# Scatter of three bfloat16 parts in one product, left terms from blocks that DMA brings into fixed slots

## What is computed

```python
idx = concatenate([edge_index, edge_index[:, ::-1]])      # 400,000 x 2
src, dst = idx[:, 0], idx[:, 1]
gl = (h @ Wl.T).reshape(N, 4, 16)[src]                    # "left" term
gr = (h @ Wr.T).reshape(N, 4, 16)[dst]                    # "right" term, gathered
score = (att * leaky_relu(gl + gr, 0.2)).sum(-1)          # 4 heads an edge
m = segment_max(score, src)
ex = exp(score - m[src])
denom = segment_sum(ex, src)
out = segment_sum(gr * (ex / denom[src]), src)            # N x 64
x = x + mlp(concatenate([out, h]))
# then: x = x + batchnorm(mlp(segment_sum(h2[src] + edge_attr, dst)))
```

## Time and profile before

| | |
|---|---|
| median of 3 runs | 9489.05 us (9473.34 to 9510.54) |
| the profiled execution's own time | 9484.91 us |
| its span | 9483.1 us |
| POOL busy | 5015.6 us (53%) |
| DVE busy | 4090.3 us (43%) |
| PE busy, PEld busy | 3658.2 us (39%), 3222.2 us (34%) |
| ACT busy | 260.2 us (3%) |
| TensorE clock granted in attention | 0.50 in every window shown below |

### The profile page before, as it was taken

How to read it: one execution, slowest core, us unless ns; L and a number is a source line. 1 busy time by engine, 2 the same in 40 slices (tenths; PEclk the granted TensorE clock), 3 DMA queues, 4 the chain that set the end, 5 groups by cost and what they waited for, 6 DMA issues and landing times. The chain is left out here.

```text
span 9483.1 us, 86794 instructions
## 1 busy us (share of the span) xinstructions
PE 3658.2 (39%) x21987; PEld 3222.2 (34%) x21988; DVE 4090.3 (43%) x6783; ACT 260.2 (3%) x352; POOL 5015.6 (53%) x4913
## 2 busy tenths in 40 slices
PE   1011112344444444444444434445463333334445
PEld 1011112343343334343333334334363333333344
DVE  8999823343444343434444344435441122222222
ACT  3011000000000000000000000000010000000000
POOL 0000065656565656556565656565417777676664
PEclk9975555555555555555555555555565555555555
DMA  2000022323232322223232223233711121111111
GB/s 21 0 0 0 26 59 68 80 78 81 69 84 74 79 76 80 72 72 83 67 88 76 77 69 83 75 77 84 66 55 46 43 45 45 44 44 44 43 44 34
DMA packets 442077, 557.62 MB, mean 59 GB/s; under 512 B 172858, under 2 KB 176058, under 8 KB 441698
## 3 DMA queue, kind: packets, MB, share of 16 engines
q1 hardware_dynamic: 281298, 391.72, 13.7%
q0 software_dynamic: 156672, 160.75, 10.8%
q10 hardware_dynamic: 3984, 3.89, 0.2%
HBM read 439.99 MB, written 115.95 MB: 59 GB/s over the span
## 5 line engine op out<-in xcount | busy, mean ns | idle before, releaser
L821 POOL DMA_INDIRECT rows<-gr_table,stage x3328 | 3385.3, 1017 | 3225.4 <-DVE stage L986 2227.2
L1303 POOL DMA_INDIRECT message<-h_table,edge_stage x1568 | 1614.7, 1030 | 783.9 <-issue 466.8
L883 PE MATMUL bank<-terms,hot_sum 128*128 128x68 f32 x6656 | 1610.3, 412 | 777.8 <-issue 753.4
L871 PE MATMUL bank<-gl_parts,hot_t 128*128 x10080 | 953.9, 236 | 2286.5 <-issue 2175.9
L883 PEld LDWEIGHTS bank<-terms,hot_sum 128*128 128x128 f32 x6656 | 1517.7, 326 | 828.8 <-issue 818.2
L871 PEld LDWEIGHTS bank<-gl_parts,hot_t 128*128 128x128 bf16 x10080 | 706.8, 127 | 2549.6 <-issue 2542.5
L1007 DVE TENSOR_TENSOR z<-bank,rows 128x512 f32<-128x512 f32 x416 | 286.6, 689 | 2761.4 <-remote 2618.6
L1330 PE MATMUL bank<-message,edge_hot 128*128 128x64 f32 x3136 | 720.4, 424 | 1463.1 <-DVE message L1375 1368.6
L1330 PEld LDWEIGHTS bank<-message,edge_hot 128*128 128x128 f32 x3136 | 683.5, 330 | 1499.9 <-DVE message L1375 1403.3
L1359 DVE TENSOR_TENSOR agg<-agg,bank 128x64 f32 x196 | 43.4, 221 | 1231.7 <-remote 737.1
L1015 DVE TENSOR_TENSOR hot_sum<-iota_row,place 128x1024 f32<-128x1024 f32 x416 | 506.8, 1218 | 25.7 <-PE bank L883 25.5
(11 more groups left out here) (254 smaller groups left out, 2320.5 us busy)
## 6 DMA issues: line engine op xcount, KB each, us to landing
place_b<-place_rows SPq DMA_DIRECT2D x422, 256.0 KB
gr_rows<-rows SPq DMA_DIRECT2D x416, 256.0 KB
rows_again<-gr_rows SPq DMA_DIRECT2D x416, 256.0 KB
rows<-gr_table,stage POOLq DMA_INDIRECT x3328
edge<-in_edge_attr SPq DMA_DIRECT2D x195, 256.0 KB
message<-h_table,edge_stage POOLq DMA_INDIRECT x1568
pen_s<-pen_rows ACTq DMA_DIRECT2D x56, 64.0 KB
gr_table<-gr SPq DMA_DIRECT2D x1, 1536.0 KB
```

The lines of the kernel that those rows point to most:

```text
L821: pool.indirect_dma_start(rows[k][:, g, :], None, m.gr_table[:, :], bass.IndirectOffsetOnAxis(stage[k][:, g:g + 1], 0)).then_inc(s_gath[k] ...
L871: last = pe.matmul(bank[slot][:, g * D:(g + 1) * D], hot_t[slot][:, g * P:(g + 1) * P], m.gl_parts[:, bass.ds(blks[g // GROUP_TILES], 1), ...
L883: last = pe.matmul(sums_of(slot, i), hot2[slot][:, g, :], terms[slot][:, g * HEADS:(g + 1) * HEADS, :].rearrange("p h w -> p (h w)"), star ...
L1303: pool.indirect_dma_start(rows[k][:, e, :], None, m.h2_table[:, :], bass.IndirectOffsetOnAxis(stage[k][:, e:e + 1], 0)).then_inc(s_gath[k] ...
```

## The change

Four edits that belong together.

1. `gl_parts` isn't kept on chip. Prepare writes it to a new HBM table `gl_table` [block, partition, 3 x 64], with three DMAs behind the store of `gr_table`. In attention SP reads two block numbers a step and loads the two blocks into one of 8 fixed slots `gl_step` (384 bytes a partition and block), six steps ahead. PE's left products read these slots at fixed addresses, and PE reads no block numbers.
2. The scatter's `terms` are split in three bfloat16 parts: ACT copies the high part, DVE subtracts it (`rest`), ACT copies the middle part, DVE subtracts it into the low part. `hot_sum` becomes bfloat16. A product of a tile then has 3 x 68 = 204 bfloat16 columns, 8 products a step, and `acc` has three sums for each block, added together once at the start of the node layer.
3. PE waits once a step (`s_parts`, or `s_hot` in the first chunk) in place of its waits on hot_t, z, terms and acc.
4. DVE's order within a step is new: z, terms and its weight column, first accumulate, hot_t, leaky, second accumulate, rest, hot_sum, weighed, stage, the low part, reduce. Several tiles share memory (`z` and `leaky` with `fore`, `weighed` and a piece of `rest` with `top`).

```diff
+        m.gl_table = nc.dram_tensor("gl_table", (BLOCKS, P, 3 * D), BF16).ap()
-        m.acc = sb("acc", [P, BLOCKS, HEADS * ACCW], F32)
+        m.acc = sb("acc", [P, BLOCKS, 3, HEADS * ACCW], F32)
-        m.gl_parts = sb("gl_parts", [P, BLOCKS, 3 * D], BF16, layer0)
...
@@ prepare, sync
-            sp.wait_ge(s_grt, 32)
+            sp.wait_ge(s_gl_parts, 1)
+            for part, piece in enumerate(gl_parts):
+                sp.dma_start(m.gl_table[:, :, part * D:(part + 1) * D].rearrange("b p f -> p b f"), piece).then_inc(s_grt, 16)
+            sp.wait_ge(s_grt, 80)
...
@@ attention
+    gl_s = [sb(f"gl_step{k}", [P, STEP_GROUPS, 3 * D], BF16, ctx) for k in range(U)]
-    hot2 = [sb(f"hot_sum{k}", [P, STEP_TILES, P], F32, ctx) for k in range(LAG)]
+    hot2 = [sb(f"hot_sum{k}", [P, STEP_TILES, P], BF16, ctx) for k in range(LAG)]
+    parts = [sb(f"parts{k}", [P, STEP_TILES, 3, HEADS * ACCW], BF16, ctx) for k in range(LAG)]
...
@@ sync
+            def load_left(q, slot):
+                for i in range(STEP_GROUPS):
+                    blk = sp.value_load(m.blk_i[0:1, bass.ds(q * STEP_GROUPS + i, 1)], min_val=0, max_val=BLOCKS - 1)
+                    sp.dma_start(gl_s[slot][:, i, :], m.gl_table[bass.ds(blk, 1), :, :].rearrange("b p f -> p (b f)")
+                                 ).then_inc(s_gl[slot], 16)
                     if part.score:
                         load_place(q + LAG + 2, (k + LAG + 2) % V)
+                        load_left(q + LAG + 2, (k + LAG + 2) % U)
...
@@ tensor
-                blks = [pe.value_load(m.blk_i[0:1, bass.ds(q * STEP_GROUPS + i, 1)], min_val=0, max_val=BLOCKS - 1)
-                        for i in range(STEP_GROUPS)]
-                pe.wait_ge(s_hot, q + 1)
-                at_least(pe, s_z, q - LAG + 1)
+                pe.wait_ge(s_gl[slot], loads * 16 * STEP_GROUPS)
                 for g in range(STEP_TILES):
                     for part in range(3):
-                        last = pe.matmul(bank[slot][:, g * D:(g + 1) * D], hot_t[slot][:, g * P:(g + 1) * P],
-                                         m.gl_parts[:, bass.ds(blks[g // GROUP_TILES], 1), part * D:(part + 1) * D
-                                                    ].rearrange("p b f -> p (b f)"),
+                        last = pe.matmul(bank[slot % LAG][:, g * D:(g + 1) * D], hot_t[slot % LAG][:, g * P:(g + 1) * P],
+                                         gl_s[slot][:, g // GROUP_TILES, part * D:(part + 1) * D],
                                          start=part == 0, stop=part == 2)
...
-            def scatter(r, slot):
-                pe.wait_ge(s_terms, r + 1)
-                at_least(pe, s_acc, STEP_GROUPS * (r - LAG + 1))
-                for i in range(STEP_GROUPS):
-                    for g in range(i * GROUP_TILES, (i + 1) * GROUP_TILES):
-                        last = pe.matmul(sums_of(slot, i), hot2[slot][:, g, :],
-                                         terms[slot][:, g * HEADS:(g + 1) * HEADS, :].rearrange("p h w -> p (h w)"),
+            def scatter(slot):
+                for g in range(STEP_TILES):
+                    last = pe.matmul(sums_of(slot, g // GROUP_TILES), hot2[slot][:, g, :],
+                                     parts[slot][:, g, :, :].rearrange("p w f -> p (w f)"),
...
+                    if part.sum:
+                        pe.wait_ge(s_parts, q - CHUNK_STEPS + 1)
+                    else:
+                        pe.wait_ge(s_hot, q + LAG + 1)
...
@@ scalar
+                    act.wait_ge(s_terms, r + 1)
+                    nc.scalar.copy(parts[k % LAG][:, :, 0, :], terms_by_tile).then_inc(s_hi, 1)
+                    act.wait_ge(s_rest, r + 1)
+                    nc.scalar.copy(parts[k % LAG][:, :, 1, :], rest[:, :, :]).then_inc(s_mid, 1)
...
@@ vector
+                        dve.wait_ge(s_hi, r + 1)
+                        dve.tensor_tensor(rest[:, :, :], terms_by_tile, parts[k % LAG][:, :, 0, :], ALU.subtract
+                                          ).then_inc(s_rest, 1)
                         dve.tensor_tensor(hot2[k % LAG][:, :, :], places, at, ALU.is_equal)
...
+                        dve.wait_ge(s_mid, r + 1)
+                        dve.tensor_tensor(parts[k % LAG][:, :, 2, :], rest[:, :, :], parts[k % LAG][:, :, 1, :], ALU.subtract
+                                          ).then_inc(s_parts, 1)
...
@@ attention_nodes
+            for w in (2, 1):
+                chain.link(dve.tensor_tensor(m.acc[:, :, w - 1, :], m.acc[:, :, w - 1, :], m.acc[:, :, w, :], ALU.add))
```

More of the change, by code:

```diff
@@ L431, in _ @@
             for part in range(3):
-                piece = m.gl_parts[:, :, part * D:(part + 1) * D]
+                piece = gl_parts[part]
                 c.link(dve.tensor_copy(piece, gl[:, :, :]))
@@ L721, in attention @@
     hot_t = [sb(f"hot_t{k}", [P, STEP], BF16, ctx) for k in range(LAG)]
-    hot2 = [sb(f"hot_sum{k}", [P, STEP_TILES, P], F32, ctx) for k in range(LAG)]
[L723 to L726, removed]
+    gl_s = [sb(f"gl_step{k}", [P, STEP_GROUPS, 3 * D], BF16, ctx) for k in range(U)]
+    hot2 = [sb(f"hot_sum{k}", [P, STEP_TILES, P], BF16, ctx) for k in range(LAG)]
+    fore = sb("fore", [P, SCAN], F32, ctx)
+    z, leaky = (fore[:, i * SW:(i + 1) * SW].rearrange("p (g f) -> p g f", f=D) for i in range(2))
+    wide = sb("wide", [P, SW + STEP_TILES * HEADS * ACCW], F32, ctx)
+    top = wide[:, 0:SCAN]
+    weighed = wide[:, 0:SW].rearrange("p (g f) -> p g f", f=D)
+    rest = wide[:, SW:].rearrange("p (g w) -> p g w", g=STEP_TILES)
+    terms = sb("terms", [P, PAIRS, ACCW], F32, ctx)
+    parts = [sb(f"parts{k}", [P, STEP_TILES, 3, HEADS * ACCW], BF16, ctx) for k in range(LAG)]
     scores = sb("scores", [P, CHUNK_TILES, HEADS], F32, ctx)
@@ L755, in attention @@
     s_place = [sem(f"s_place{k}") for k in range(V)]
+    s_gl = [sem(f"s_gl{k}") for k in range(U)]
     s_hot = sem("s_hot")
+    s_hi, s_rest, s_mid, s_parts = sem("s_hi"), sem("s_rest"), sem("s_mid"), sem("s_parts")
     s_step = sem("s_step")
@@ L849, in _ @@
                 load_place(q, q % V)
+                load_left(q, q)
             def turn(part):
@@ L926, in _ @@
             for q in range(LAG):
-                left(q, q).then_inc(s_step, 1)
+                pe.wait_ge(s_hot, q + 1)
+                left(q, 1).then_inc(s_step, 1)
             def turn(part):
@@ L948, in _, with body @@
             load_pens(0)
+            def body(part, j, first):
+                if not part.sum:
+                    return
+                for k in range(U):
+                    r = U * j + k - CHUNK_STEPS
+                    act.wait_ge(s_terms, r + 1)
+                    nc.scalar.copy(parts[k % LAG][:, :, 0, :], terms_by_tile).then_inc(s_hi, 1)
+                    act.wait_ge(s_rest, r + 1)
+                    nc.scalar.copy(parts[k % LAG][:, :, 1, :], rest[:, :, :]).then_inc(s_mid, 1)
             def turn(part):
                 c = part.c
+                if part.sum:
+                    loop(act, part, body)
                 if not part.score:
@@ L1008, in body @@
                                           rows[k][:, :, :], ALU.add).then_inc(s_z, 1)
+                    if part.sum:
+                        weight = weights[:, bass.ds(tile, STEP_TILES), :].rearrange("p g h -> p (g h)")
+                        dve.wait_ge(s_load[k % V], place_loads(j - outer, k))
+                        dve.tensor_tensor(terms[:, :, 0:DH],
+                                          rows2[k % V][:, :, :].rearrange("p g (h f) -> p (g h) f", f=DH),
+                                          weight.unsqueeze(2).to_broadcast([P, PAIRS, DH]), ALU.mult)
+                        dve.tensor_copy(terms[:, :, DH:ACCW], weight.unsqueeze(2)).then_inc(s_terms, 1)
+                    if add:
+                        accumulate(r - LAG, k % LAG, 0)
+                    if part.score:
                         hot_of(q + LAG, k % LAG, (k + LAG) % V, place_loads(j, k + LAG))
```

55 lines of the change are left out of this document (27 added, 28 removed).

## The result

The changed kernel takes 9341.44 us (median of 4 runs, 9317.39 to 9365.21) where the kernel before takes 9484.07 (4 runs beside them): a ratio of 0.9845, 95% interval 0.9805 to 0.9886. Forecast were 9325. The profiled execution took 9319.15 us, span 9317.3. So 166 us went between the two profiled executions, 143 between the medians, where 162 were forecast. But the parts of that sum came out quite different, so that the agreement is luck, and the last experiments make it likely that the sign itself hangs on a condition that lies outside the kernel.

A forecast was written before the change was run, and what follows sets the result against it. POOL was taken to wait for DVE and DVE for PE, slow at starting instructions. 9484.9 - 109 (short waits) - 240 (chunk ends) + 104 (gathers) + 83 (fixed costs) = 9323, rounded 9325 us; range 8550 to 9810.

The forecast's parts named there:

- What bounds the kernel: Attention: POOL waits for DVE, DVE for PE, which lacks its rate of starting instructions; 1,263 us of waits.
- I take a quick stretch to end after so many PE records, not after a time: Attention: a quick stretch holds 240 PE records, so 3.75 steps at 64 records, and a cycle grows from four steps to 5.7.
- the rival's fixed time: Attention: PE is quick for 16 us in all, to about 8 us after POOL's restart, whatever it has to start; chance 0.30.
- my -109: POOL's short waits for stage inside chunks: 74 become 52 at 10.6 us each, 551 us for 660.
- Chunk ends: POOL's waits at the 12 chunk ends: 20 us less each, -240 us in all, 0 to -500 possible.
- Gathers: POOL's gathers stretched by the two subtracts: +0.25 us a step, +104 us over 416 steps.
- Fixed costs: Prepare +15, memset and sum additions +12, last chunk +20, wider accumulations and longer last step at chunk ends +36: +83 us.
- Hidden work: ACT's copies (0.56 us each, up to 0.7) and SP's gl loads: nothing added to the time.
- The crawl is gone: Rival, chance 0.24: without the register-addressed operand PE no longer crawls in attention and POOL bounds all, 8579 us.
- POOL held up by DVE: Rival, chance 0.10: the two subtracts delay gathers by their whole length, 570 us for 104, total 9789 us.
- the likeliest: Main case, chance 0.36: fewer crawls, cycles of 5.7 steps, 9323 us, own range 9050 to 9480.
- Slower: Rival, chance 0.30: quick stretches are bounded by time, DVE fits 2.3 steps in place of 3, 9839 us.

The follow-up runs named there:

- e3: The changed kernel with 8 more bfloat16 products a step whose sums nobody reads, 80 records instead of 64: 9429.84 us, ratio 0.9807 to the kernel before.
- e6: The changed kernel's order, single wait and left slots, but float32 scatter products, no parts, copies or subtracts: 9605.59 us, ratio 0.9984 to the kernel before.
- e8: The changed kernel with VectorE's two subtracts cut to 8 columns each: 9446.95 us, ratio 0.9782 to the kernel before.
- e11: The kernel before, with POOL clearing 320 columns of an unused tile after every second gather: 8835.05 us, ratio 1.0758 to the kernel before (8213.67 us there).
- e1: The kernel before with only the left part changed (gl blocks by DMA into fixed slots): 9613.63 us, ratio 1.0007 to the kernel before.
- e2: The changed kernel with TensorE's left operand again addressed by registers, read from memory twice a step: 9437.84 us, ratio 0.9814 to the kernel before.
- e12: The changed kernel with subtracts cut to 8 columns each and two 512-column reduces of a constant in their places: 8425.48 us, ratio 1.0243 to the kernel before.
- e5: The kernel before with hot_sum and terms as bfloat16 tiles, leaving out the terms' middle and low part: 9328.58 us, ratio 0.9674 to the kernel before.
- e9: The kernel before, with POOL clearing a few bytes of an unused tile after every second gather: 9564.82 us, ratio 0.9955 to the kernel before.

## Why the forecast held, and where it did not

The time was right (9325 for 9341) and the sign was right. That the time is so near is luck: four terms were off by 285, 153, 182 and 53 us, some one way and some the other. The mechanism was half right. Point by point:

- *What bounds the kernel.* Right: the wait that ended last was POOL for VectorE for PE, and PE lacked a rate of starting instructions, not work time. What I did not see is that SyncE, and VectorE when it has work, share the beat. I had named the mark by which I would be wrong in the main: PE's issue waits not following its records. They did not (2176 and 2164 us; 2101 in e3).
- *The step that failed* is "I take a quick stretch to end after so many PE records, not after a time". In the changed kernel neither it nor the rival's fixed time is so: 16 more records change nothing (e3), and quick stretches went from 16 us to about 90. There a crawl begins when VectorE has caught up with POOL: behind the first chunk POOL is about one step ahead or less at its start. That is no rule for the kernel before, whose crawls begin with POOL nearly five steps ahead and 14 us after its restart; there the forecast's count of records and the rival's fixed time both still stand. So the forecast took the changed kernel to keep the old kind of quick stretch, and it went over to another. What brings that about is shown only in part: it took both the bfloat16 products (e6 without them keeps the short cycle, but has 80 records and no subtracts too) and the two subtracts at full length (e8). Why, stays open. Hence -394 us for my -109.
- *Chunk ends.* -87 us for -240. A crawl almost always falls on the chunk's last steps, so VectorE comes into the scan nearly as late as before (waits of up to 49 us, where the kernel before had up to 54).
- *Gathers.* The kind was right, the size was not: +286 us for +104. The next fence shows why: VectorE's two-operand work of a step stands nearly in a row, and this gather, started beside it, ends only when the row does.

```profile
3793.12 0.99 POOL L836 DMA_INDIRECT rows<-gr_table,stage  x1 [0.30 <-issue]
...
3794.13 1.21 DVE L1064 TENSOR_TENSOR hot_sum<-iota_row,place 128x1024 bf16<-128x1024 f32 x1
...
3794.41 2.36 POOL L836 DMA_INDIRECT rows<-gr_table,stage  x1 [0.30 <-issue]
3795.27 0.68 DVE L1067 TENSOR_TENSOR wide<-fore,att_sb 128x512 f32<-128x512 f32 x1
3795.87 0.16 DVE L1020 TENSOR_SCALAR stage<-row_of 128x8 int32 x1
3795.94 0.71 DVE L1073 TENSOR_TENSOR parts<-wide,parts 128x544 bf16<-128x544 f32 x1
3796.58 0.67 DVE L136 TENSOR_REDUCE scores<-wide 128x512 f32 x1
```

  The gather of 3794.41 ends at 3796.77, just past the end of the low part's subtract (3796.65) and inside the reduce that follows, which reads one operand. It is no single case: of the 378 gathers over 1.3 us, 281 end 0.1 us behind the low part's subtract. Beside no VectorE work a gather takes 0.94 us in both kernels (mean of 1606 after, of 1998 before); beside some, 1.25 us in the changed one, 1.13 before. My 0.58 us from 3.3 us of such work is 0.18 us a us; the same ratio is 0.27 here, 1.28 us from 4.7. The Trainium skill (SBUF — State Buffer, "SBUF: two separate sides") says that such an operation and a GpSimd one lock each other out wholly; this fence agrees with it better than the 0.94 to 1.43 on which I doubted it.
- *Fixed costs.* +30 us for +83. Prepare: nothing, not +15; the casts to bfloat16, whose output is no longer strided, took 1.79 us each and not 3.42, and the stores were through by 184, ahead of POOL's next work at 189.83. Last turn: 3.91 us a step for my 4.0 (3.41 before).
- *Hidden work.* Right: ScalarE's copies (0.645 us) made VectorE wait 2.8 us in all, the gl loads made PE wait in three places, 48 us. VectorE's quick step is 6.5 us where I had 7.0 (two starts of z, written to `fore`):

```profile
3790.65 0.67 DVE L1041 TENSOR_TENSOR fore<-bank,rows 128x512 f32<-128x512 f32 x1
...
3797.18 0.67 DVE L1041 TENSOR_TENSOR fore<-bank,rows 128x512 f32<-128x512 f32 x1
```

- *The rivals.* "The crawl is gone" gave 8579 us. The change did not do that; a condition outside the kernel seems to have: 8214 us for the kernel before, unchanged, and no crawl in e11 beside it. Register addresses, which I gave that rival as its reason, are not needed for a crawl (the changed kernel has none and crawls), do not bring one by themselves (e11 has them and does not), and do not set the cycle (e1, e2). "POOL held up by DVE" put 570 us on the gathers, the likeliest 104; with 286 the truth lies between. "Slower" named the time since POOL's restart; for the changed kernel that failed, 100 us for its 8.

Where there is no crawl, the change has next to nothing to win, and what it costs stays: longer gathers and a longer last turn. e12, which has all of the change but reduces for the subtracts (it leaves out the low part and most of the middle one) and gathers of 1.116 us, is 2.4% slower than the kernel before there. The changed kernel itself was not run in that condition; with gathers of 1.104 us it should come out near e12, slower than before by 2 to 3%, which is an estimate.

## What to carry to other kernels

A gain that comes from fewer waits for a stalled engine is only worth what the stall is worth where the kernel will run; time the kernel before in several jobs before trusting it. When a wait is cured, look at how the engine behind it is paced: here the gathers, held up by two-operand VectorE work in a row, gave back 286 of 481 us. And test the cheap half of a change by itself: the left slots brought nothing, the bfloat16 tiles alone 3.3%, though with two of the three parts of the terms left out.

## What the runs showed that was not expected

- The same kernel took 9484 to 9625 us in four jobs and 8214 in a fifth, each time with a spread under 1%. There is no trace of it in the fifth. If what follows attention's gathers took as long there as in e11 (2481 us, where the kernel before has 2682), some 200 us of the difference lie there and 1070 in attention, where e11 has no crawl; this is an estimate.
- In a crawl of the changed kernel TensorE, SyncE and VectorE start instructions on one beat of 0.70 us while GpSimd keeps its pace of 1.25 us a gather; it ends within some 9 us of GpSimd's stop.
- Crawls come in two kinds: 7 to 14 us after GpSimd's restart with GpSimd four to five steps ahead, or some 90 to 100 us after it with GpSimd one step ahead or less.
- With float32 products (80 records a step) GpSimd's waits come back after 3 or 4 steps, with bfloat16 ones (64 records) after 5 to 10 (the kernel before and e5), though the clock is 0.50 in both and TensorE is busy for 44% and 26% of the time between 1650 and 6500 us.
- A GpSimd clear of 0.12 us between two gathers costs nothing, as it lies inside the 0.30 us of issue before the next one (e9).
